# A decoder's cross attention: row maxima, their transposes and the value projection at other steps of the schedule

## The reference, cut to what matters

```python
q = x @ w_q + b_q                # 16 x 256 x 128
k = context @ w_k + b_k          # 16 x 1601 x 128
v = context @ w_v + b_v
scores = jnp.einsum('bqhd,bkhd->bhqk', q, k) * scale
weights = jax.nn.softmax(scores, axis=-1)
out = jnp.einsum('bhqk,bkhd->bqhd', weights, v).reshape(B, Lq, D) @ w_o + b_o
x = layernorm(x + out)
```

## Time and profile before

| | us |
|---|---|
| median of 3 executions (3858.93 to 3862.2) | 3859.53 |
| the profiled execution's own time | 3866.06 |
| its span in the trace | 3864.3 |

### The profile page before, as it was taken

How to read it: one execution, slowest core, us unless ns; L and a number is a source line. 1 busy time by engine, 2 the same in 40 slices (tenths; PEclk the granted TensorE clock), 3 DMA queues, 4 the chain that set the end, 5 groups by cost and what they waited for, 6 DMA issues and landing times. The chain is left out here.

```text
span 3864.3 us, 97882 instructions
## 1 busy us (share of the span) xinstructions
PE 3442.3 (89%) x39003; PEld 1703.8 (44%) x39003; DVE 2871.3 (74%) x3920; ACT 2329.9 (60%) x4575; POOL 1067.8 (28%) x1874
## 2 busy tenths in 40 slices
PE   5885999999999999984999582999999999999988
PEld 3442444444444444433666581444444444444435
DVE  5776788888888888854344896888888888888852
ACT  3663677777777777771332530777777777777663
POOL 4552223222222322201665002232222223222201
PEclk9997999999999999996999795999999999999998
DMA  3332222232222223201000002222322222232200
GB/s 98 75 79 58 61 55 60 55 77 61 56 63 54 59 58 75 57 12 25 1 0 1 0 0 61 53 60 56 76 63 54 63 54 59 62 70 63 49 16 22
DMA packets 165138, 194.88 MB, mean 50 GB/s; under 512 B 32166, under 2 KB 124123, under 8 KB 164715
## 3 DMA queue, kind: packets, MB, share of 16 engines
q1 hardware_dynamic: 164714, 189.03, 20.8%
HBM read 27.88 MB, written 2.10 MB: 8 GB/s over the span
## 5 line engine op out<-in xcount | busy, mean ns | idle before, releaser
L586 ACT ACTIVATE cross_Pr<-cross_sT 128x512 f32<-128x512 f32 (+1 forms) x3584 | 1833.6, 563 | 768.8 <-PE cross_sT L508 767.8
L649 DVE TENSOR_REDUCE cross_nm<-cross_ring 128x2 f32<-128x802 f32 x2048 | 1975.6, 991 | 323.7 <-PE cross_ring L474 295.3
L508 PE MATMUL cross_sT<-cross_Q,cross_K 64*128 64x256 bf16 x13312 | 1044.2, 273 | 49.3 <-ACT cross_Pr L586 42.2
L527 PE MATMUL cross_oT<-cross_Pr,cross_V 128*9 128x256 f32 x13312 | 1029.8, 381 | 0.0
L508 PEld LDWEIGHTS cross_sT<-cross_Q,cross_K 64*128 64x128 bf16 x13312 | 511.1, 95 | 771.8 <-ACT cross_Pr L586 637.1
L474 PE MATMUL cross_ring<-cross_K,cross_Q 64*128 64x401 bf16 x4096 | 662.3, 337 | 62.2 <-DMA cross_K<-cross_kparts 33.5
L401 POOL TENSOR_TENSOR cross_mp<-cross_nm,cross_one 128x8 bf16<-128x8 f32 x128 | 25.9, 202 | 1373.6 <-DVE cross_nm L654 1373.6
L527 PEld LDWEIGHTS cross_oT<-cross_Pr,cross_V 128*9 128x9 f32 x13312 | 197.6, 88 | 412.6 <-issue 245.1
L474 PEld LDWEIGHTS cross_ring<-cross_K,cross_Q 64*128 64x128 bf16 x4096 | 199.0, 94 | 202.7 <-DVE cross_nm L649 106.9
L1104 DVE TENSOR_TENSOR moe_rc<-moe_r,moe_bank 128x512 f32<-128x512 f32 x128 | 87.9, 687 | 170.8 <-ACT moe_r L995 170.8
L876 POOL TENSOR_TENSOR moe_hh<-moe_r,moe_rc 128x512 f32<-128x512 f32 x128 | 162.5, 1270 | 160.0 <-DVE moe_rc L1104 159.3
(11 more groups left out here) (296 smaller groups left out, 3035.7 us busy)
## 6 DMA issues: line engine op xcount, KB each, us to landing
cross_K<-cross_kparts SPq DMA_DIRECT2D x1152, 100.1 KB, 2.3
cross_in<-in_ctx_T_dram SPq DMA_DIRECT2D x32, 600.4 KB, 5.5
self_QK<-self_parts SPq DMA_DIRECT2D x144, 128.0 KB, 2.7
cross_Q<-cross_qparts SPq DMA_DIRECT2D x288, 64.0 KB, 2.1
X<-in_x_dram SPq DMA_DIRECT2D x4, 512.0 KB, 6.1
self_in<-in_x_T_dram SPq DMA_DIRECT2D x16, 128.0 KB, 2.3
cross_Q<-cross_mst SPq DMA_DIRECT2D x128, 16.0 KB, 1.8
out_dram<-X SPq DMA_DIRECT2D x1, 2048.0 KB, 8.7
```

Source lines behind the costliest of these rows:

```text
L508: mm = pe.matmul(sT[0:r, cfg.sT_bank(b, u + j), (c % 2) * S:(c % 2 + 1) * S], K[ROWS * j:ROWS * (j + 1), pair, t, s:s + r], Q[ROWS * j:ROW ...
L527: mm = pe.matmul(oT[32 * j:32 * j + VR, 0:S], V[0:r, b % VB, c, 4 * g + j, :], Pr[0:r, slot, (c % 2) * S:(c % 2 + 1) * S], start=(c == 0), ...
L586: act.activation(Pr[0:r, u % NPR, 0:nc_ * S], sT[0:r, cfg.sT_bank(b, u), 0:nc_ * S], ACT.Exp).then_inc(exped, 1)
L649: dve.tensor_reduce(nm4[:, g % 2, t, :, pk, blk], R.rearrange("p (j n) -> p j n", j=2)[:, :, 0:cfg.block], AX.X, ALU.max, negate=True).the ...
```

## The change

It moves units of the cross attention in `_schedule` and changes one wait. Nothing is computed that was not computed before.

```diff
             for g in range(QUADS):
-                out += [(g * u - u - 6 + (a * u + 2) // 16, ("A", g, a)) for a in range(16)]
-                out += [(g * u - 4, ("MT", g)), (g * u - 3, ("ROWS", g))]
-            out += [(-s + 1, ("XT", 0)), (-s + 4, ("Q", 0)), (-s + 4, ("SPLIT_Q",)), (-s + 12, ("STACK_Q",))]
-            out += [(-s + at, ("K", n)) for n, at in enumerate((9, 11, 13))]
-            out += [(-s + (9, 11, 13)[self.split_of[j]], ("SPLIT_K", j)) for j in range(len(self.ksplit))]
-            out += [(-s + at, ("V", n)) for n, at in enumerate((48, 52, 55))]
-            out += [(-s + at, ("STACK_K", g)) for g, at in enumerate((27, 30, 44, s + 1))]
+                out += [(g * u - 2 * u + (a * u + 10) // 16, ("A", g, a)) for a in range(16)]
+                out += [(g * u - u + 2, ("MT", g)), (g * u - u + 3, ("ROWS", g))]
+            out += [(-s + 1, ("XT", 0)), (-s + 3, ("Q", 0)), (-s + 3, ("SPLIT_Q",)), (-s + 9, ("STACK_Q",))]
+            out += [(-s + at, ("K", n)) for n, at in enumerate((4, 6, 8))]
+            out += [(-s + (4, 6, 8)[self.split_of[j]], ("SPLIT_K", j)) for j in range(len(self.ksplit))]
+            out += [(at, ("V", n)) for n, at in enumerate((0, 5, 10))]
+            out += [(-s + at, ("STACK_K", g)) for g, at in enumerate((22, 30, 44, s + 1))]
             out += [(-2 * s + 27, ("LOAD_C",))]
-            bias, ox, ont, fin, ln = 2, (32, s + 3), s + 5, s + 7, s + 9
+            bias, ox, ont, fin, ln = 2, (32, s + 17), s + 19, s + 21, s + 23
@@
                         if n_ == 0:
                             if b * QUADS + g > 0:
                                 pe.wait_ge(o_out, gq)
-                            if g == 0:
-                                pe.wait_ge(by["dve"], cfg.read(i, "V", (len(cfg.chunk_units) - 1,), off))
+                        for unit, (lo, _) in enumerate(cfg.chunk_units):
+                            if g == 0 and lo in cfg.bursts[n_]:
+                                pe.wait_ge(by["dve"], cfg.read(i, "V", (unit,), off))
```

## The result

The changed kernel takes 3885.88 us (3882.8 to 3888.58, 6 runs), the kernel before, run again beside it, 3859.89. The ratio is 1.0066, interval 1.0053 to 1.0079: slower by 26 us, clear of the 0.2% that can be told from no change. Forecast were 3877, with a range of 3856 to 3893, and "slower".

The account below looks back on a forecast made before the run. TensorE, busy 89%, bounds it, with a 1.29 us floor of B, exponential, B. Terms gave 9.8 us a layer, 19.6 for both, taken as +17.5: 3877 us, eight-in-ten range 3856 to 3893.

Parts of the forecast that it names:

- (1) MT: MT into the step without PV: gives back 0.47 in three groups, 0.11 in the first; -1.52 us an iteration.
- (2) The second A: Second A moved from a free step into half step 12: +0.35 us a group, +1.40 an iteration.
- (3) V and K: V1's and K0's waits go (-0.51, -0.50), new waits at steps 5 and 11 (+0.42, +0.32): net -0.27 us.
- (4) OX1, ONT, OUT: One group later: ONT waits 0.42 at double step 19, next A 0.06, OX0's follower 0.17; +0.65 us an iteration.
- the steady one: Inner iterations, fourteen a layer: moves sum to +0.26 us each, bounds -1.4 to +0.7; +3.6 a layer.
- the signs that the text gave for being right: MT steps 1.30, half steps 1.37 and 1.10, PV waiting 0.3, ONT 0.4, iteration 84.0 to 84.4, last iteration +3 to 4.
- (5) The ends: Each layer: +1.3 us ahead of the first B, +3.7 in the last iteration, +1.4 for the slow clock.
- (6) DMAs and GpSimd: Key stack DMAs, ROWS and key splits, costed at nothing; about 5 us of slack stay before A needs STACK_K0.
- a doubled A in a half step hides: Rival: second A in step 12 of each group costs nothing, 32 x 1.40 = -45 us, giving 3832; chance 0.13.
- MT not hiding: Rival: MT costs 0.2 in its new step, +26 us, 3903; chance 0.05 together with a late key stack.
- a late key stack: Rival: STACK_K0 or key splits end 1 us late, +32 us, 3909; chance 0.05 together with MT not hiding.
- the slower queue: Rival: queued VectorE reductions 0.99 apart, some eight waits grow by 0.09 each, +22 us, 3899; chance 0.02.

Follow-up runs that it names:

- the spread version of the changed kernel: Changed kernel with double steps at 4 and 10 of a group and XT, Q, K, V, OX0, OX1, ONT, OUT, LN moved: 3833.15 us, ratio 0.9926.
- both runs made from the kernel before: Kernel before, second A at step 5 instead of 9: 3829.52 us; the same with ONT, OUT, LN, OX0, V1 moved off double steps: 3808.31 us.

## Why the prediction was right

**(1) MT.** Right in sign and size: steps 10 and 11 of a group gave back 0.47 where nothing else was near, and MT's new step takes 1.29. The reason was wrong in the main: the text put the 0.47 down to MT. The runs show that 0.36 of it belonged to the double step in front of MT (18.39 - 18.03 with only that step moved). The change moved it away as well, so that the term came out right is luck. MT's own part is 0.1 a group, and its new place takes as much back, 1.41 instead of 1.30 in the step behind it; beside a V unit MT costs more, 3.18 - 2.57 = 0.61. That the step behind the new place stays at 1.41 because A, MT, A need the ring as A, A, A did is shown by MT's return to step 10, where it falls to 1.30.

**(2) The second A.** Forecast +0.35 a group, measured 1.40 + 1.09 - 2.12 = +0.37. The picture of a dear half step was too narrow: in the full step before a half one the second A costs 0.13 + 0.21, in full steps with slack behind them 0.14.

**(3) V and K.** Step 5 took 2.97; the terms of the forecast give 1.44 + 1.05 + 0.42 = 2.91. Step 11 took 1.69, and they give 1.30 + 0.32 = 1.62. The 0.50 at K0 is borne out by the run that moved only the double step: step 9 fell from 2.99 to 2.32, of which 0.15 is the second A itself and 0.52 the wait.

**(4) OX1, ONT, OUT.** The waits of ONT and of the A behind it were put at 0.42 + 0.06 = 0.48; taking ONT out of the double step gave 0.45 for the two steps. OX0's follower took 1.57 against 1.44 + 0.17 = 1.61. The third group, where (1), (2) and the wait for OX0's reader meet, was to grow by -0.47 + 0.35 + 0.17 = 0.05 and did, from 18.94 to 18.99.

**The term that was too small** is the steady one: +0.52 an iteration in place of +0.26. Of the missing 0.26, 0.14 is the last step of an iteration: 735.35 - 734.11 = 1.24 in place of 1.10. Its PV begins as usual, and the next B comes 0.15 late with no engine named; before, V2's matmuls stood there. It is 1.23 to 1.24 in each of the five kernels whose step 55 has no V, though step 54 is a double step in some, follows one in others, and in the spread version of the changed kernel is an ordinary half step of 1.06. So the ring is not its cause, and what it is stays open. Of the rest, 0.07 is PV's wait and 0.06 step 5; smaller differences nearly cancel. Of the signs that the text gave for being right, only the iteration missed: 84.55 against 84.0 to 84.4. An error of 0.26 is as large as the steady term itself, the small remainder of terms of 1.5 and 1.4, so that its sign came out right is in part luck; the ends, 12.4 of the 19.6 us forecast, were the firmer part. Rounding the sum down to 17.5 because "my walk rounds waits upwards" was wrong: it rounded them down.

**(5) The ends.** The last iteration is right to the tenth, the first and the stretch ahead of it within 0.4 each. The run with V back splits that stretch: nine A cost 7.9 (forecast 8.1), and V's leaving gave 7.0 (forecast 6.7). The windows that follow show the slow clock reaching further than before. First the kernel before, then three of the changed one:

```profile
400.00:404.00 4.00, 4.00 (x48) 1.73 (x44) 3.71 (x5) 2.50 (x6) 0.03 (x1) 0.96 0.01 2
```

```profile
396.00:400.00 4.00, 3.53 (x20) 2.13 (x20) 3.63 (x5) 1.08 (x2) 0.92 (x5) 0.50 0.02 6
400.00:404.00 4.00, 4.00 (x28) 1.98 (x26) 1.75 (x3) 1.76 (x4) 0.57 (x1) 0.50 0.00 0
404.00:408.00 4.00, 3.97 (x41) 1.69 (x40) 3.05 (x4) 2.83 (x7) 0.71 (x2) 0.86 0.02 4
```

The first B stands at 397.11 here (394.48 before). Ahead of it TensorE did A units at the lower level, 1.2 GHz; the granted clock was still 0.50 from 400 to 404 us, where it was 0.96 before, and 0.86 in the next four.

**(6) DMAs and GpSimd.** Costed at nothing, and in the list of waits of the changed kernel they cost an inner iteration nothing. The DMA ROWS brought something that the text did not count; the last section has it.

**The rivals.** That a doubled A in a half step hides is refuted (1.40, not 1.06); so are MT not hiding (1.29), a late key stack (no A of an inner iteration waits for a DMA) and the slower queue. On the rule of the Trainium skill, page "VectorE: DVE Perf Modes", section "The DRAIN you can't avoid": queued reductions start 0.90 apart here too, and a walk with that spacing met the steps named above within 0.07. The rule taken literally is not what this kernel does. But the same section adds that a next operation that is not held starts earlier, and the 0.90 fits that exception, which the prediction left out; its "the trace does not agree" holds for the rule without it only.

## What to carry to other kernels

Where engines share a two-deep PSUM ring in program order, cut the timeline at a unit that occurs once in each step and write down the price of every kind of step; a hand walk with four latencies then gave most new steps within 0.07, and missed by 0.14 the one that it had no pattern for. Before moving a unit that looks dear, look at its neighbours: here 0.36 of its 0.47 belonged to the doubled unit in front of it, and moving only that unit gained more (ratio 0.9917, with its followers spread 0.9859) than the whole change lost (1.0066). Keep a step with two units for the slower reader (here two A for VectorE) away from short steps and from the step before them, and from steps with other ring units; and put more than one step between a unit that is copied and the unit that needs the copy.

## What the runs showed of the hardware that was not expected

A small DMA (16 KB, a median of 1.8 us from issue to landing) was late often enough to matter. In the kernel before ROWS has three steps until B needs it. In the profiled execution five of its inner iterations are longer than 84.03, by 0.67, 1.63, 0.38, 0.62 and 0.35. The list of its waits, the times to landing of all 128 ROWS, and rows of TensorE's timeline at the end of such a group name the DMA:

```profile
PE cross_sT L508 <- DMA cross_Q<-cross_mst: 3.3, 6, 0.9
```

```profile
DMA to landing us min/median/max: 1.7/1.8/4.0
```

```profile
1276.10 0.41 PE L508 MATMUL cross_sT<-cross_Q,cross_K 64*65 64x256 bf16 x4
...
1277.84 0.61 PE L508 MATMUL cross_sT<-cross_Q,cross_K 64*128 64x256 bf16 x8 [0.61 <-DMA cross_Q<-cross_mst]
```

This ROWS was issued at 1274.04, as usual, and landed 3.8 us later. In the changed kernel ROWS leads by eleven steps; the wait is gone from its list, and its inner iterations lie within 0.03 us of each other. The wait is there again in the run with MT back at step 10 and in both runs made from the kernel before; it is gone in all four runs in which ROWS kept its eleven steps. It does not look random: in the kernel before and in both runs made from it the late ones fall in iterations 11 and 12 of the first layer and 4 and 5 of the second, counted from 0 (in the kernel before also in 10 of the first). What delays them there stays open. The five longer iterations add up to 3.65 us, about the 3.5 by which the two profiled spans (22.5 us apart) are closer than the medians (26.0 apart); that other executions of the kernel before lose less to it is not shown.
